# GELU expert stages: the first-layer weight copy of the next tile moves ahead on VectorE, and each finished tile is scattered to token order by one indexed DMA

## What is computed

```python
logits = xf @ gate_w + gate_b                       # 1024 tokens, 8 experts
top_val, top_idx = jax.lax.top_k(logits, 2)
gate_score = jax.nn.softmax(top_val, axis=-1)
comb = einsum('tk,tke->et', gate_score, one_hot(top_idx)) * alpha[:, None]
for e in range(8):                                  # fc1 256 -> 1024, fc2 1024 -> 256
    h = gelu(xf @ fc1_w[e] + fc1_b[e])
    out = out + (h @ fc2_w[e] + fc2_b[e]) * comb[e][:, None]
x = x + 0.5 * out
```

## Time and profile before

| | us |
|---|---|
| median of three runs | 2405.76 |
| the three runs | 2404.11, 2405.76, 2411.33 |
| the profiled execution: its own time | 2403.5 |
| the profiled execution: its span | 2401.8 |
| PE busy | 2025.8 (84%) |
| DVE busy | 1286.1 (54%) |
| ACT busy | 1000.3 (42%) |
| POOL busy | 391.6 (16%) |

### The profile page before, as it was taken

One profiled execution on the slowest core, in us unless ns is written; L12 is line 12 of the kernel. 1 busy time (PEld: TensorE's weight loads), 2 busy tenths in 40 slices (PEclk: granted clock), 3 DMA queues, 4 the chain that ended last, 5 costly groups with the idle time before them and its releaser, 6 DMA issues. The chain is left out here.

```text
span 2401.8 us, 52328 instructions
## 1 busy us (share of the span) xinstructions
PE 2025.8 (84%) x20606; PEld 1490.4 (62%) x20606; DVE 1286.1 (54%) x2928; ACT 1000.3 (42%) x2476; POOL 391.6 (16%) x442
## 2 busy tenths in 40 slices
PE   7889898788626689999999999999999998858884
PEld 4544455677514467767776776777677667638774
DVE  4435444212234576777667767766776776431222
ACT  2114421222113445664665566556546654512221
POOL 0002100200200122212221222122122212202102
PEclk9969998899856899999999999999999999958997
DMA  1100003710101111011101110110111010045001
GB/s 46 33 13 1 15 26 105 250 31 21 44 11 45 30 31 24 18 35 24 33 20 37 24 33 20 33 27 18 35 24 33 20 28 11 11 164 187 27 21 62
DMA packets 148345, 100.08 MB, mean 42 GB/s; under 512 B 88640, under 2 KB 134992, under 8 KB 148112
## 3 DMA queue, kind: packets, MB, share of 16 engines
q1 hardware_dynamic: 144368, 86.59, 12.8%
q0 software_dynamic: 3744, 10.23, 1.5%
HBM read 83.28 MB, written 13.50 MB: 40 GB/s over the span
## 5 line engine op out<-in xcount | busy, mean ns | idle before, releaser
L1589 PE MATMUL dn_ps<-xnT,dn_w 128*128 128x512 f32 x512 | 260.5, 635 | 35.2 <-DMA dn_w<-in_W_qkvz_dram 23.9
L1942 DVE SCALAR_TENSOR_TENSOR dn_cv<-dn_raw,dn_cw,dn_cv 128x1024 f32<-128x1024 f32 x192 | 270.6, 1409 | 1.2
L588 PE MATMUL g_ps<-g_w,xnT 128*128 (+1 forms) x736 | 166.1, 379 | 0.0
L1589 PEld LDWEIGHTS dn_ps<-xnT,dn_w 128*128 128x128 f32 x512 | 91.2, 197 | 116.3 <-issue 100.1
L577 PE MATMUL g_ps<-g_xT,g_w_now 128*128 128x128 f32 x960 | 117.4, 282 | 50.3 <-DVE g_w_now L716 50.3
L1734 PE MATMUL dn_ps<-dn_wout,dn_oT 128*128 128x256 f32 x512 | 150.0, 418 | 6.2 <-ACT dn_oT L1749 3.7
L1749 ACT ACTIVATE dn_kdk<-dn_ps,dn_cf 128x128 f32<-128x128 f32 x256 | 80.2, 364 | 179.3 <-PE dn_ps L1629 179.3
L516 ACT ACTIVATE xnT<-g_ps,g_b_now 128x128 f32<-128x128 f32 x240 | 68.6, 368 | 206.1 <-PE g_ps L577 206.1
L577 PEld LDWEIGHTS g_ps<-g_xT,g_w_now 128*128 128x128 f32 x960 | 112.6, 196 | 61.5 <-issue 61.5
L588 PEld LDWEIGHTS g_ps<-g_w,xnT 128*128 128x128 f32 x736 | 136.4, 190 | 16.7
L1749 ACT ACTIVATE dn_raw<-dn_ps 128x512 f32<-128x512 f32 x128 | 76.6, 598 | 148.7 <-PE dn_ps L1589 148.7
(11 more groups left out here) (309 smaller groups left out, 4413.2 us busy)
## 6 DMA issues: line engine op xcount, KB each, us to landing
g_w<-in_fc_dram SPq DMA_DIRECT2D x32, 1024.0 KB, 13.1
dn_w<-in_W_qkvz_dram SPq DMA_DIRECT2D x16, 768.0 KB, 4.5
dn_x<-dn_cum_rows SPq DMA_DIRECT2D x32, 256.0 KB, 3.9
ys_rows<-g_ys SPq DMA_DIRECT2D x46, 128.0 KB, 1.7
dn_wout<-in_W_out_dram SPq DMA_DIRECT2D x16, 256.0 KB, 2.8
f_gate<-in_gateT_dram SPq DMA_DIRECT2D x16, 128.0 KB, 2.2
f_up<-in_upT_dram SPq DMA_DIRECT2D x16, 128.0 KB, 2.4
f_down<-in_downT_dram SPq DMA_DIRECT2D x16, 128.0 KB, 2.4
```

The costliest lines, as they stand in the source:

```text
L588: last = pe.matmul(y_b[i % 2][:, 0:D], hT[i % 2][:, f, :], of(f), start=(f == 0), stop=(f == NF - 1))
L1589: mm = pe.matmul(to, w[:, k, W_COL[u] * P:(W_COL[u] + 1) * P], m.xnT[:, k, b * T:(b + 1) * T], start=(k == 0), stop=(k == KD - 1))
L1942: ins = nc.vector.scalar_tensor_tensor(out=cv[:, u], in0=raw[:, u, :, tap:tap + T], scalar=cw[:, g, tap:tap + 1], in1=cv[:, u], op0=ALU.mu ...
```

## The change

Three things change, all in `moe_gelu`, for both stages.

1. In DVE's tile loop `copy_w1(i + 1)` is issued first, ahead of `copy_x(i + 2)` and `copy_y(i - 1)`.
2. `place_u` has one index per slot of a tile in place of one per pick: token + 1024 r for a used slot, row 2048 (SPARE) for an empty one. It comes from a third block of `token` and a wider PE product. When tile i is done, POOL scatters its 128 rows by one indexed DMA straight to these rows (`put_back`); SP no longer stores tiles. The scatter of tile i waits until that of tile i - 1 has landed.
3. At the end SP, not POOL, issues 16 plain DMAs that read `ys_rows` in order. DVE's four bias additions come ahead of the weighted additions.

```diff
-SLOTS = TILES * P
+R_BACK = R_TILE + 2 * NT
+R_WIDTH = R_BACK + 2 * NT
+SPARE = 2 * NTOK
...
+    back = (SPARE - NTOK * (np.arange(2 * NT) // NT)).astype(np.float32)
...
-            for i in range(TILES):
-                sp.wait_ge(y_copied, i + 1)
-                sp.dma_start(tile_rows(ys_rows, i), ys[:, i % 3, :]).then_inc(ys_stored[i % 3], 16)
+            sp.wait_ge(y_copied, TILES)
             for n in range(3):
                 sp.wait_ge(ys_stored[n], 16 * ((TILES - n + 2) // 3))
+            for t in range(NT):
+                for r in range(2):
+                    sp.dma_start(gathered[r][:, t, :], tile_rows(ys_rows, r * NT + t)).then_inc(ys_back[t], 16)
...
+            def put_back(i):
+                pool.wait_ge(y_copied, i + 1)
+                if i >= 1:
+                    pool.wait_ge(ys_stored[(i - 1) % 3], 16 * ((i + 2) // 3))
+                nc.gpsimd.indirect_dma_start(ys_rows, bass.IndirectOffsetOnAxis(ap=place_u[:, i:i + 1], axis=0),
+                                             ys[:, i % 3, :], None).then_inc(ys_stored[i % 3], 16)
+
+            for i in range(RING):
+                fetch(i)
             pool.wait_ge(place_ready, 1)
-            for n in range(3):
-                pool.wait_ge(ys_stored[n], 16 * ((TILES - n + 2) // 3))
-            for t in range(NT):
-                for r in range(2):
-                    j = r * NT + t
-                    nc.gpsimd.indirect_dma_start(gathered[r][:, t, :], None, ys_rows,
-                                                 bass.IndirectOffsetOnAxis(ap=place_u[:, j:j + 1], axis=0)).then_inc(ys_back[t], 16)
+            for i in range(TILES):
+                if i + RING < TILES:
+                    fetch(i + RING)
+                put_back(i)
...
-                last = pe.matmul(y_b[0][:, 0:2 * TILES], in_slot[:, j, :], token[:, j].rearrange("p a n -> p (a n)"),
+                last = pe.matmul(y_b[0][:, 0:3 * TILES], in_slot[:, j, :], token[:, j].rearrange("p a n -> p (a n)"),
...
+            nc.vector.tensor_tensor(token[:, :, 2, :], in_tile[:], over_tiles(route[:, R_BACK:R_BACK + 2 * NT]), ALU.mult).then_inc(token_ready, 1)
...
-            chain(nc.vector.scalar_tensor_tensor(out=place_f[:], in0=tile_f[:], scalar=float(P), in1=slot[:], op0=ALU.mult, op1=ALU.add))
-            nc.vector.tensor_copy(place_u[:], place_f[:]).then_inc(place_ready, 1)
...
+            chain(nc.vector.scalar_tensor_tensor(out=place_f[:], in0=in_tile[:, 0, :], scalar=float(SPARE), in1=in_tile[:, 1, :],
+                                                 op0=ALU.add, op1=ALU.add))
+            nc.vector.tensor_tensor(place_u[:], place_f[:], in_tile[:, 2, :], ALU.subtract).then_inc(place_ready, 1)
...
             for i in range(TILES):
+                if E1 <= i + 1 < TILES:
+                    copy_w1(i + 1)
                 if i + 2 < TILES:
                     copy_x(i + 2)
                 if i >= 1:
                     copy_y(i - 1)
-                if E1 <= i + 1 < TILES:
-                    copy_w1(i + 1)
             copy_y(TILES - 1)
+            for g in range(4):
+                dve.wait_ge(b2_ready, g + 1)
+                two = m.x[:, 2 * g:2 * g + 2, :].rearrange("p t d -> p (t d)")
+                nc.vector.tensor_tensor(two, two, h_b[g], ALU.add).then_inc(b2_added, 1)
             for t in range(NT):
-                if t % 2 == 0:
-                    dve.wait_ge(b2_ready, t // 2 + 1)
-                    two = m.x[:, t:t + 2, :].rearrange("p t d -> p (t d)")
-                    nc.vector.tensor_tensor(two, two, h_b[t // 2], ALU.add).then_inc(b2_added, 1)
```

More of the change, by code:

```diff
@@ L342 @@
 R_PART, R_TILE = R_SLOT + P, R_SLOT + P + 1
-R_WIDTH = R_TILE + 2 * NT
+R_BACK = R_TILE + 2 * NT
+R_WIDTH = R_BACK + 2 * NT
+SPARE = 2 * NTOK
 def route_constants():
@@ L359, in route_constants @@
     tile = np.tile(P * np.arange(NT), 2).astype(np.float32)
+    back = (SPARE - NTOK * (np.arange(2 * NT) // NT)).astype(np.float32)
     spread = lambda a: np.broadcast_to(a, (P, len(a)))
     part = r[:, None].astype(np.float32)
-    return np.ascontiguousarray(np.concatenate([before, ones, groups, count, spread(rows), part, spread(tile)], axis=1))
+    return np.ascontiguousarray(np.concatenate([before, ones, groups, count, spread(rows), part, spread(tile), spread(back)], axis=1))
 def moe_gelu(nc, m, tag, gate, gate_bias, fc1, fc1_b, fc2, fc2_b, alpha, iota_in, route_in, xn_rows, ys_rows):
@@ L392, in moe_gelu @@
         held = sb("held", [P, 2 * NT, E1])
-        rank_f, tier, slot, held_first, tile_f, place_f = (sb(n, [P, 2 * NT]) for n in (
-            "rank_f", "tier", "slot", "held_first", "tile_f", "place_f"))
+        rank_f, tier, slot, held_first, tile_f = (sb(n, [P, 2 * NT]) for n in (
+            "rank_f", "tier", "slot", "held_first", "tile_f"))
         above = sb("above", [P, 2 * NT, E1 - 1])
-        place_u = sb("place_u", [P, 2 * NT], U32)
+        place_f = sb("place_f", [P, TILES])
+        place_u = sb("place_u", [P, TILES], U32)
         in_slot = sb("in_slot", [P, 2 * NT, P], BF16)
         in_tile = sb("in_tile", [P, 2 * NT, TILES])
-        token = sb("token", [P, 2 * NT, 2, TILES], BF16)
+        token = sb("token", [P, 2 * NT, 3, TILES], BF16)
         token_u = sb("token_u", [P, TILES], U32)
@@ L481, in _, with fetch @@
             pool.wait_ge(tokens_ready, 1)
-            for i in range(TILES):
+            def fetch(i):
                 if i >= RING:
@@ L539, in _ @@
             pe.matmul(y_b[1][:, P:P + E1], totals[:], route[:, R_GROUP + P:R_GROUP + P + E1], start=True, stop=True).then_inc(ranks_ready, 1)
-            pe.wait_ge(token_ready, 2)
+            pe.wait_ge(token_ready, 3)
             for j in range(2 * NT):
@@ L679, in _ @@
                                         route[:, None, R_SLOT:R_SLOT + P].broadcast_to([P, 4, P]), ALU.is_equal).then_inc(in_slot_ready, 1)
-            chain(nc.vector.scalar_tensor_tensor(out=place_f[:], in0=tile_f[:], scalar=float(P), in1=slot[:], op0=ALU.mult, op1=ALU.add))
-            nc.vector.tensor_copy(place_u[:], place_f[:]).then_inc(place_ready, 1)
             dve.wait_ge(tokens_found, 1)
-            chain(nc.vector.tensor_copy(in_tile[:, 0:2, :], y_b[0][:, 0:2 * TILES].rearrange("p (a n) -> p a n", a=2)))
+            chain(nc.vector.tensor_copy(in_tile[:, 0:3, :], y_b[0][:, 0:3 * TILES].rearrange("p (a n) -> p a n", a=3)))
             nc.vector.tensor_tensor(token_u[:], in_tile[:, 0, :], in_tile[:, 1, :], ALU.add).then_inc(tokens_ready, 1)
@@ L2086, in build @@
         load_inputs(nc, m, a["x"], const(a["c_table"], C_EYE))
-        xn_rows, ys_rows = (nc.dram_tensor(f"{n}_rows", (rows, D), F32).ap() for n, rows in (("xn", NTOK), ("ys", SLOTS)))
+        xn_rows, ys_rows = (nc.dram_tensor(f"{n}_rows", (rows, D), F32).ap() for n, rows in (("xn", NTOK), ("ys", SPARE + P)))
         for s in stages:
```

## The result

The changed kernel takes 2326.16 us (median of four runs, 2323.9 to 2328.95) against 2404.94 us for the kernel before (four runs, 2401.44 to 2411.33): a ratio of 0.967, 95% interval 0.9647 to 0.9693. That is 78.8 us less. The forecast was 2327 us.

The account below looks back on a forecast made before the run. Bounds: PE's wait for weight copies behind result copies, and POOL's return gathers at stage end. 30.4 + 29.8 + 2 x 9.8 - 2 x 0.5 = 78.8 us off 2405.8 gives 2327 us, range 2320 to 2343.

Parts of the forecast that it names:

- The step that carried three quarters of the sum: Tile loop: weight copy no longer waits behind the result copy; gains 30.4 us in stage 3, 29.8 in stage 5.
- the period of the static tiles: Tile loop: first layers of tiles 8 to 22 come 7.25 us apart, as in tiles 0 to 7, not 9.11.
- PE's own reading of the owner's number: Tile loop: the next possible late event on PE; started last 5.4 us before tile 22's first layer needs it.
- Tile 8's clock: Tile 8's first layer: 1.63 us of slow clock counted as gained, since the gap before it is gone.
- Routing: Before `in_slot`, on the path to the first gather: one more product costs 0.5 us a stage, ends 0 and 1.
- The scatters: Tile loop: issue near 0.96 us, landing taken as 3.6 us, waits covered by later work.
- The slower case: Scatters of empty tiles: writes to one row taken one after another, about 0.10 us per row loses the gain; chance 3%.
- The return: Stage end: SP's plain loads replace POOL's 16 return gathers, then 8.3 us of DVE additions; gains 9.8 us a stage.
- its low end: Whole kernel: landing 2.7 us, no routing cost and run scatter give about 2321 us; 2320 taken.
- A new small wait of PE: First layers of tiles 8 to 22: half the old wait stays, 0.8 us x 30 tiles, 24 us: 2351; chance 6%.
- Slow scatters: Stage end: landings of 6.6 us, 11.8 us less gain, 2339 us; or loads sharing DMA engines worse, 2337; chance 12%.
- One part without effect: Whole change: for instance the weight copy gains nothing because PE waits for something else, 2387 us; chance 1%.

Follow-up runs that it names:

- The new order alone: The kernel before with only the next tile's weight copy issued first in VectorE's tile loop: 2347.9 us against 2412.5, ratio 0.973.
- the run with the scatters alone: The changed kernel with VectorE's old loop order (weight copy last): 2390.7 us against 2412.5 for the kernel before, ratio 0.991.
- the run with own rows: The changed kernel with each empty slot p sent to row 2048 + p instead of all to row 2048: 2334.7 us in one run.
- two queues: The changed kernel with separate rows for empty slots and ScalarE issuing the second picks' return loads: 2325.3 us against 2408.6 for the kernel before, ratio 0.9654.
- the run with the weight copy second: The changed kernel with the weight copy between `copy_x(i + 2)` and `copy_y(i - 1)` in VectorE's loop: 2328.4 us in one run.

## Why the prediction was right

The 78.8 us agree to the tenth by chance, since the four runs of either kernel lie 5 and 10 us apart. The stages are the better measure: 79.1 us less, and the mechanism shows in their parts.

**The weight copy.** The step that carried three quarters of the sum held at every point: the place of the wait, the period of the static tiles as what remains, nothing new behind it. Stage 5's stretch from tile 6's second layer to tile 22's first took 2192.70 to 2297.47, 104.8 us, reckoned 105.0. PE's own reading of the owner's number did not show up, as its lead had said. The new order alone gives 60.6 us of the 79.1 that the two profiled stages lose.

**Tile 8's clock.** Counting the 1.6 us a stage as gained was right for this kernel, but the reason was too simple. I took the fall for a consequence of tile 8's gap; the runs show gaps of 2.0 to 2.4 us with and without it. That these first layers see no fall where there is no gap is what holds in all profiles; it is no rule for PE's other work (see the bias products below).

**Routing.** The extra product (L687) took 0.45 us in the chain of waits of the changed kernel, 0.5 was taken:

```profile
2123.01 0.45 DVE g_token L686
2123.46 0.45 DVE g_token L687
2123.90 2.42 DVE g_in_slot L690 x4
```

In the run with the scatters alone it took 0.4 us (stage 3) and 0.3 us (stage 5) longer than before from a stage's first DMA to tile 7's first layer, so the whole of routing cost no more than the 0.5 us.

**The scatters.** Their issue takes 0.98 us in the loop, as that of a gather. All 46 land in a median of 2.5 us (2.4 to 4.2), the last ones in 3.1, where 3.6 was taken and 2.7 to 6.6 allowed. Reading the slow landing as that of one row named 128 times was confirmed by the run with own rows. Nothing in the tile loop was held up by their waits. The slower case had its mechanism, at less than a fifteenth of the price at which it decides (0.006 against 0.10 us a write).

**The return.** Set against the last result copy, the forecast put the second scatter's issue 1.1 us behind it, its landing 4.7, the first load 4.8, the first addition 7.5 and the end 15.8 us. Measured: 1.1, 4.2, 4.7, 7.3 and 16.3. Two terms were off, and against each other: each of the two landings was 0.5 us better, and the handovers were longer than reckoned, 0.7 us from a landing to the next scatter where 0.3 was taken and 0.5 us from the landing to SP's first load where 0.1 was. And DVE's additions took 9.0 us, not 8.3: two pairs came 0.3 us late and a third 0.1 us. SP issues a pair in 0.95 us and DVE adds one in 1.04 us, so the loads gain only 0.1 us a pair on the additions, while the second picks landed in 2.1 to 3.2 us. The forecast's 7.1 us for moving 2 MB was near: with two queues 2.1 MB moved at 322 GB/s in that stretch, which makes 6.5 us. By itself the return gives 9.4 us in stage 5 and 9.9 in stage 3, reckoned 9.8.

**The range.** 2326.16 us lies well inside 2320 to 2343. The terms of its low end give 2321.7 us (2327 less 2.6, 1 and 1.7), where the forecast has "about 2321"; nothing hangs on it.

**The rivals.** A new small wait of PE: none. Slow scatters: none. One part without effect: refuted by the two half changes, 60.6 and 20.3 us by their stages, of which 1.6 us of the second are a clock that happened not to fall.

## What to carry to other kernels

In a queue that one engine works off in order, a copy that depends on an early event must not stand behind one that waits for a late one. The price, paid each turn, is the part of the delay that no slack covers: here 1.86 us (9.11 less 7.25). Once the copy was ahead, it was done 2.7 us before it was needed. It is enough to pass the one instruction that waits late, as the run with the weight copy second shows. And a permutation that must be done at the end of a stage can be paid in the loop, if the engine that issues it has room there (POOL, 2.4 us of each 7.25), so that the end only reads in order. Before a second queue is given to such reads, the DMA engines' share in that stretch should be looked up: here it was 0.87 already, and the second queue made the stages no shorter than own rows alone.

## What the runs showed of the hardware

**A weight copy on VectorE holds up GpSimd's issue of a DMA.** A token gather is issued in 0.97 us when no weight copy runs (the weight copy second, 2194.02), in 1.17 us where it starts halfway through one (order alone, 2205.63 beside 2205.28), and in 1.45 us where it starts 0.1 us into one (changed kernel, 2194.72 beside 2194.62); it costs nothing here, as POOL has room. The Trainium skill (SBUF — State Buffer, section SBUF: two separate sides) describes such a lock for copies from SBUF to SBUF and the writing of descriptors; the traces agree, with a price of up to 0.48 us on the gather; the other way round the price is smaller, as a weight copy took at most 0.77 us for 0.69 (0.82 in the run with the scatters alone). It had not been part of the forecast, as before the change no weight copy met a gather (none took over 0.70 us).

**Many writes to one DRAM row.** 128 rows of 1 KB to one place land 0.7 us later than to 128 places, 3.1 against 2.4 us.

**Two issuing queues fill the DMA engines.** 2 MB of return loads from two queues keep them busy for 0.99 of 6 us, at 322 GB/s; from one queue it is 0.87 and 258 GB/s, and each load lands sooner (2.4 to 2.8 us, not 3.8 to 4.6).

**The same bias products at the end of a stage take 3.7 to 5.3 us.** In the changed kernel they took 3.72 us in stage 5 (granted clock 1.00 from 2304.0 to 2309.3) and 4.92 us in stage 3 (0.79 from 614.1 to 620.5), and with two queues 5.34 us in stage 5 (0.68 from 2306.0 to 2311.5). PE had stood idle for 0.24 us before them each time, also where they took 3.72 us, so that gap does not tell them apart; what does stays open.
